# Moving the slots of the projections, the front layer norm and the value rows in two attention stages of a one-core decoder kernel

## What is computed

```python
# L0_ffn, its first half ("f0"): layer norm in front, biases, no norm behind
hn = _layernorm(x, ln1_g, ln1_b)
q, k, v = hn @ wq + bq, hn @ wk + bk, hn @ wv + bv      # split into 16 heads of 8
attn = softmax(q @ k.T / sqrt(8)); x = x + (attn @ v) @ wo + bo
# L1_attn ("a1"): root-mean-square norm of q and k per head, layer norm behind
q, k, v = rms_norm(x @ Wq.T, qn_w), rms_norm(x @ Wk.T, kn_w), x @ Wv.T
x = layernorm(x + (softmax(q @ k.T * 8**-0.5) @ v) @ Wo.T)
```

## Time and profile before

| | us |
|---|---|
| median of 3 runs (5181.83 to 5212.17) | 5211.31 |
| run of the profiled execution | 5181.83 |
| its span | 5180.0 |
| f0, from first to last row maximum | 439.8 |
| a1, from first to last row maximum | 498.9 |

### The profile page before, as it was taken

The page is one execution under the profiler, slowest core; times in us unless marked ns, Lnnn a source line. Parts: engine busy times, 40 slices in busy tenths (PEclk is TensorE's granted clock), DMA queues, the critical chain, the costliest instruction groups (busy, mean ns, idle before and its releaser), DMA issues. The chain is left out here.

```text
span 5180.0 us, 104514 instructions
## 1 busy us (share of the span) xinstructions
PE 4003.7 (77%) x29689; PEld 2315.3 (45%) x29692; DVE 4107.7 (79%) x8425; ACT 2798.1 (54%) x6477; POOL 2805.9 (54%) x3454
## 2 busy tenths in 40 slices
PE   5888787787788778887588868998193888889953
PEld 2333333333333333333366646666182666657732
DVE  5988888998888899888488877886144888868878
ACT  4555555555555555554477754445274555445535
POOL 5766666676666666666377753334443222234345
PEclk8988888898898898888699989997596999989975
DMA  2101111110111111111255535655113555455521
GB/s 88 70 35 72 72 44 65 72 72 35 72 72 39 70 72 59 48 72 39 61 104 107 108 74 118 130 126 171 51 57 103 108 110 110 87 125 124 120 53 33
DMA packets 320686, 420.40 MB, mean 81 GB/s; under 512 B 40512, under 2 KB 302225, under 8 KB 309649
## 3 DMA queue, kind: packets, MB, share of 16 engines
q1 hardware_dynamic: 316048, 408.35, 30.2%
q0 software_dynamic: 4352, 8.95, 0.5%
HBM read 307.65 MB, written 109.58 MB: 81 GB/s over the span
## 5 line engine op out<-in xcount | busy, mean ns | idle before, releaser
L1861 PE MATMUL bank<-m_h,ident 128*128 128x512 f32 x2048 | 1254.3, 707 | 408.5 <-DVE m_h L2127 355.2
L2228 POOL TENSOR_TENSOR m_h<-m_dtu,m_Bb 128x512 f32<-128x512 f32 x1024 | 1321.7, 1318 | 330.4 <-PE bank L1861 324.9
L2121 DVE TENSOR_TENSOR_SCAN m_h<-bank,m_h 128x512 f32<-128x512 f32 x1024 | 1246.3, 1217 | 201.2 <-ACT bank L2009 192.1
L2009 ACT ACTIVATE bank<-m_dt,m_A 128x512 f32<-128x512 f32 x1024 | 695.6, 688 | 757.2 <-DVE m_h L2121 671.5
L1861 PEld LDWEIGHTS bank<-m_h,ident 128*128 128x128 f32 x2048 | 391.0, 215 | 1072.9 <-DVE m_h L2127 862.4
L2127 DVE TENSOR_TENSOR m_h<-m_h,bank 128x512 f32<-128x512 f32 x1024 | 676.5, 661 | 1.9 <-PE bank L1854 1.7
L547 ACT ACTIVATE x_sm<-bank,x_nm 128x77 f32<-128x77 f32 x1024 | 318.2, 336 | 60.1 <-DVE x_nm L712 58.4
L712 DVE TENSOR_REDUCE x_nm<-bank 128x4 f32<-128x308 f32 x512 | 238.7, 474 | 129.4 <-PE bank L370 123.2
L1805 PE MATMUL bank<-m_xTp,m_wck 128*128 128x512 f32 x512 | 265.5, 623 | 11.9 <-ACT m_xTp L1923 11.9
L537 ACT ACTIVATE f_pT<-bank 128x512 f32<-128x512 f32 x256 | 153.0, 598 | 204.6 <-PE bank L390 203.4
L537 ACT ACTIVATE a_pT<-bank 128x512 f32<-128x512 f32 x256 | 153.1, 599 | 176.9 <-PE bank L390 174.7
(11 more groups left out here) (425 smaller groups left out, 9788.4 us busy)
## 6 DMA issues: line engine op xcount, KB each, us to landing
m_Bb<-m_B SPq DMA_DIRECT2D x32, 4096.0 KB, 12.2
x_Ks<-x_k_parts SPq DMA_DIRECT2D x64, 231.0 KB
x_q_parts<-x_qp SPq DMA_DIRECT2D x32, 384.0 KB, 3.9
x_Qs<-x_q_parts SPq DMA_DIRECT2D x32, 384.0 KB
f_Ks<-f_k_parts SPq DMA_DIRECT2D x32, 384.0 KB
a_Ks<-a_k_parts SPq DMA_DIRECT2D x32, 384.0 KB
x_xp<-x_stage SPq DMA_DIRECT2D x32, 256.0 KB
x_Qs<-x_q_parts SPq DMA_DIRECT2D x32, 256.0 KB
```

The source lines that it names most:

```text
L1861: pe.matmul(banks[4 + c], ident[:], h[:, k % RING, :], start=(s == 0), stop=(s == NS - 1)).then_inc(s_ya.sem, 1)
L2009: act.activation(decays[k % AHEAD], dt[:, d, c, :], ACT.Exp, scale=A[:, d, c, s:s + 1]).then_inc(s_dA.sem, 1)
L2121: v.tensor_tensor_scan(h[:, k % RING, :], decays[k % AHEAD], h[:, k % RING, :], 0.0, ALU.mult, ALU.add).then_inc(s_h.sem, 1)
L2228: pool.tensor_tensor(h[:, k % RING, :], dtu[:, d, c, :], Bb[:, d, s, :], ALU.mult).then_inc(s_dB.sem, 1)
```

## The change

The places z of some pieces change; no instruction is added or removed. `norm_at` and the `ln` line serve f0 only, the `rms` line a1 only; x0 and x1 use the last line, which stays.

```diff
-    norm_at = (-12, -8, -4, -3)
+    norm_at = (-12, -11, -8, -7)
     if rms:
-        slot = {"x": -12, "qt": -11, "kt": -8, "qn": -2, "kn": -1, "v": 0}
+        slot = {"x": -11, "qt": -10, "kt": -9, "qn": -2, "kn": -1, "v": 3}
         later = {"v": 1, "high": 2, "middle": 3}
         squares_at, root_at, inverse_at, norm_slots = (-8, -7), -6, -4, (-3, -2)
     elif ln is not None:
-        slot, later = {"x": -2, "q": -1, "k": 0, "v": 3}, {"v": 3, "high": 1, "middle": 2}
+        slot, later = {"x": -6, "q": -5, "k": -4, "v": 3}, {"v": 3, "high": 1, "middle": 2}
```

## The result

| | before | after |
|---|---|---|
| median of the runs (us) | 5210.49 (4 runs, 5181.83 to 5212.17) | 5262.85 (4 runs, 5259.41 to 5272.27) |
| profiled execution | 5181.83 | 5254.81 |
| f0, first to last row maximum | 439.8 | 469.2 |
| a1, first to last row maximum | 498.9 | 525.4 |

The changed kernel takes 1.0117 times as long, 95% interval 1.0086 to 1.0149. That is slower by over 1%, and above the predicted range (5180 to 5238, chance of "slower" 0.05).

What follows compares the result with a forecast made beforehand. PE was taken to set the pace in f0, losing 2.4 us a group to late DVE or ACT; in a1 the two share the work. f0 plus 1 and a1 plus 5 made plus 6: 5217 us on the median, range 5180 to 5238.

Steps and rivals of the forecast that it cites:

- the walk: f0, one group slot by slot: waits sum to 3.0 us against 2.4, plus 0.6 a group, plus 7 over 12 groups.
- the wait is 0.9: f0, slots 0 and 1: PE waits 0.9 us for DVE's late residual add, before 0.33, since v no longer hides it.
- Stacks: f0: stored parts are ready a sequence earlier, so PE's waits for the stack go: minus 4 us.
- prologue: Ahead of f0's loop: k of group 1 and four casts fit under DVE's 10.3 us idle; first turn loses them, minus 3.
- SP: SP's DMA order stays, parts and output store are issued earlier, copies have about 13 us of room: no effect.
- loop: f0, the loop's way back on DVE comes free from under a PE wait: below 1 us, 5 times, plus 1.
- kt in slot 7 instead of 8 is free, DVE has 2.6 us of work there: a1, slot 7: making kt one slot earlier costs nothing, as DVE has 2.6 us of work there.
- The new wait of x behind the value copy: a1, slot 5: x needs the bank that the v copy in slot 4 frees late, a new PE wait of 0.85 us.
- plus 0.4 a group: a1: PE and the maximum of slot 7 come 0.3 to 0.45 us later, passed on; plus 5 over 13 groups.
- rival 1: DVE's heavy slots are spread and lateness goes, f0 and a1: minus 20 to minus 35 us, within 1%, chance 0.27.
- rival 3: f0's loop, moved in the program, is fetched again each turn: plus 15 us, 5232 in all, chance 0.1.
- rival 4: New PE waits bring the clock down in 12 more groups: plus 56 us, 5267 or above, slower by over 1%, chance 0.05.

Runs made afterwards that it cites:

- e4: Only the f0 part of the change, with POOL's bias add moved behind the spread of the value rows, against the kernel before: 5200.84 us, ratio 0.9998.
- e10: Only the a1 part of the change, but ACT squares and copies kt in slot 8, behind `ou`, against the kernel before: 5195.08 us, ratio 0.9997.
- e7: Only the a1 part of the change, with kt back in slot 8, against the kernel before: 5200.01 us, ratio 0.9993.
- e8: Only the a1 part of the change, with v back in slot 0 and its copy in slot 1, against the kernel before: 5235.92 us, ratio 1.0067.
- e1: The kernel before, unedited, timed and profiled once more: 5205.75 us, ratio 0.9996.
- e2: Only the f0 part of the change (the rms line goes back), against the kernel before: 5229.16 us, ratio 1.0046.
- e3: Only the a1 part of the change (`norm_at` and the `ln` line go back), against the kernel before: 5233.88 us, ratio 1.0053.
- e6: The f0 part alone plus 24 unread 128x128 bf16 products ahead of L378 in slot 1, against the kernel before: 5213.93 us, ratio 1.0020.

## Why the prediction was wrong

**f0, the walk: right but for one term.** The waits that the prediction walked through, beside those of the changed kernel: slot 6 `nmT` 0.4, measured 0.24; slot 7 turn of the weighed output 0.3, 0.30; slot 9 L378 0.6, 0.60; slot 10 `nmT` 0.4, 0.16; slot 12 `ou` 0.4, 0.38; norm behind POOL's power 0.4, 0.58. Two of them, of PE:

```profile
3245.23 0.33 PE L426 MATMUL bank<-ident,f_on 128*128 128x128 f32 x1 [0.30 <-DVE f_on L744]
...
3247.51 0.22 PE L378 MATMUL bank<-identb,f_nmp 128*48 128x128 bf16 x1 [0.60 <-DVE f_xr L755]
```

**The step that failed in f0** is "the wait is 0.9" in slots 0 and 1. It was 1.70, and a fall of the clock, for which the sum had no term, came with it: 0.8 + 1.4 = 2.2 us a group beyond the walk. The 0.9 took DVE's durations from the kernel before. They depend on what POOL does at that moment, and the walk never put POOL's queue through the new order; of POOL's instructions it moved only those that the diff names. e4, which puts the bias add elsewhere, measures 0.70 there and shows the walk's time of a group.

**Stacks, prologue, SP, loop.** The wait of PE for the stacks is gone (2.6 us before), SP's order cost nothing that the waits show, and x0 is unchanged. f0's first group was no shorter (26.7 beside 25.5 us), so the prologue's 3 us did not come at the start. They came at the end: the k piece and the casts that the prologue takes over are missing in group 14, which takes 22.1 us in e4 beside 26.0 (the last L340 starts at 3508.7 us before the change, in group 14, and at 3531.2 after it, in group 13). The last two groups of e4 take 42.4 us beside 46.3. The sum forecast for f0, plus 1, stands beside e4's 435.0 against 439.8 and 441.1: minus 5 or 6, within what an untouched stage varies by. The loop's other groups were 0.2 to 0.6 us longer in e4 than in the kernel before, where the walk has 0.6.

**The step that failed in a1** is "kt in slot 7 instead of 8 is free, DVE has 2.6 us of work there". It looks at DVE, and for DVE and PE it holds (e10). But the piece also moves on ACT's queue, from behind `ou` to ahead of it, with 1.2 us of work. PE's wait of 0.86 us for it and the falls of the clock that come with it (14 instead of e7's 6, 1.4 us each) are the loss; e7 and e10 take it away, e8 does not. Which pause brings which fall is not shown: the falls begin in slot 5, ahead of the wait in slot 8, or in slots 12 and 13, behind the roots' wait of 1.90 us, and that wait is there in e7 too, with a fall and without. The new wait of x behind the value copy came as forecast: the terms given (2.2 - 1.45) make 0.75, not the 0.85 of the text, and 0.72 was measured. The forecast of plus 0.4 a group shows in e7, which has this change and not the loss: its groups without a fall take 30.8 us, such groups 30.3 in the kernel before and 30.2 in e1. That e7's a1 is all the same 501.2 us long, against e1's 503.3, where plus 5 was forecast, is luck: it has 6 falls outside slot 1 from group 1 to 13, e1 has 11.

**The rivals.** The lateness did not go (rival 1): it halved for `nmT` and came back at L378. Code was not fetched again in each turn of f0's loop (rival 3): the changed kernel shows no instruction packets there between 3245 and 3500 us. But "f0's loop shows no such queue" was not so for the first turn of the kernel before, which has three q8 instruction packets between 3180 and 3210 us. The clock (rival 4) is what came, with a chance of 0.05: it was priced at 4.7 us a group and 56 in all, by one group of the earlier trace rows, and came at 1.4 us a fall, in every loop group of f0 and in most of a1. The price was misread: that group holds the pause of 2.84 us shown above, ahead of the fall, so PE had not been at work "with only short waits", and 2.84 of the 4.7 us are not the clock's. The chance was too small because the argument was "the total of the waits grows little". The total is not what the clock followed. With L378's wait of 1.70 us the clock fell in 14 of 14 groups of the changed kernel and in 11 of 14 of e2; with 0.70 in its place (e4) in none. In the kernel before, with waits of 1.1 us and less, it fell in 2 further groups of f0. What decides over a single fall was not found.

**What was to show it.** `nmT` fell by 42%, not by more than half; L378 rose over 15, to 30.1, where the walk's 0.6 and 0.9 over 12 groups are 18; f0 left 435 to 446; the waits of L333 (10.0 us) and of `a_vS` and the places of L343 came as said. The wait for `ou` rose to 41.2, but 13 waits of 0.78 to 0.86 us, 11 us in all, stand in slot 8, and the 30 left are near 32. Both bounds for "wrong" (f0 by 12, a1 by 10) were passed. The third, a change of x1, would have misled: e1 has the long x1 without any edit.

**The sum.** 28.1 and 22.1 us against e1's trace is 50.2, of 52.4 between the medians. In f0 the changed kernel has 14 falls (20 us) and 14 times 0.8 us of wait beyond the walk (11), the walk's own 0.6 over 13 groups is 8, and the first group is 1.3 longer. Off it go what e1 has and the changed kernel has not: 4 falls (6 us), the pause in the first turn (2.6) and the k piece and casts of group 14 (4.8, by e4's). That leaves 27 of the 28.1. In a1, against e7's 501.2, the wait is 13 x 0.86 = 11 of 24 us and the clock 8 x 1.4 = 11. One bound of the range was also added up wrongly: rival 1's minus 35 on the median of 5211 is 5176, not 5180; the measured 5263 lies above the other end. Left open: why the changed kernel's a1 (525.4) had fewer falls of the clock than e3's (538.6) with the same code for a1 (14 beside 22, outside slot 1 and from group 1 to 13), and what makes x1 long or short.

## What to carry to other kernels

When a step moves in an engine's list, redo the order of every engine's queue that holds a part of it, and look at what stood behind it: that instruction moves too, though no line of the diff names it. Put the new POOL order beside the new DVE order, since here a small operation of two SBUF inputs lasted to the end of the POOL operation beside it (1.19 us instead of 0.17). And weigh a new wait of PE by its own length and what follows, not by the total: a repeated pause of 1.7 us cost 1.4 us more in the clock behind it in most groups. Before a group is taken as the price of something, look whether it holds a pause of another kind.

## What the runs showed of the hardware

- **A short DVE operation beside a long POOL one.** L719 reads two SBUF tiles of 16 columns: 0.17 us alone, 1.19 us beside POOL's 1.26 us add, and in all 14 cases it ended 0.03 us after it. L717, a cast, took 0.63 instead of 0.17 beside `low` and ended with it too, before the change as well. The row maxima, which read PSUM, kept to 0.69. The Trainium skill (Advanced Engine Details and Errata, GPSIMD Details) says that the Pool engine shares a read and a write interface with DVE, in conflict with DVE operations that have two SBUF inputs or run in a 2-port mode. The traces agree for L719, and put the price at all that is left of the POOL instruction; whether the cast ran in such a mode no run here shows.
- **The clock after one pause.** Behind L378's pause of 1.70 us the granted clock was 0.57 over 4 us with PE busy for 3.92 of them, then 1.00 again; it cost 1.4 us a group (e6 against e2, and e2's own groups with and without a fall). Three groups of e2 had the same pause (1.50 to 1.74 us) and no fall. In a1 a fall in slot 1 cost nothing (30.8 us with and without it in e7). Products that nobody needs, put into the pause, kept the clock at 1.00.
- **Pauses of PE that nothing ends, and instruction packets.** In x1, with the same code, an execution had 18, 27 or 36 packets of the q8 instruction queue and took 435.7 to 439.2, 445.5 to 449.1 or 454.4 to 463.3 us; with 18 L370 had one such pause of 9.9 us, with 36 (e1) five with 20.3 us in all. e6, with 24 products more in the loop, had nine such packets between 3245 and 3500 us, where e2 had none, and two groups of 5 to 7 us more. That PE stood because its instructions came late fits this, but no run tested it.
